# The start of a state-space and mixture-of-experts kernel: one convolution chunk moved to TensorE, three small steps moved

## The chip, the cores and the metric

The kernel is one program on one core of a Trainium2 chip. The metric is the device time of a run in microseconds. Lower is better.

## What is computed

The input x has 4 batches of 256 rows and 256 channels. It goes through a selective state-space layer (driven by a context, gated by the normalised x) with a residual, and then through a layer of 8 experts, top 2, with a residual. The part that matters here is what precedes the recurrence:

```python
x = jnp.einsum('ed,bld->bel', in_proj_w, hidden_states)      # 128 -> 256 channels
xc = conv(pad(x, 3), conv_w)                                 # 4 taps, one filter per channel
u = silu(xc + conv_b)
x_dbl = jnp.einsum('ke,bel->bkl', x_proj_w, u)               # dt_lo (8), B (16), C (16)
delta = softplus(dt_proj_w @ dt_lo + dt_proj_b)
A = -exp(A_log)
# 256 steps: state = state*exp(delta*A) + (delta*u)*B;  y = state . C
y = (y + D * u) * silu(layernorm(x))
```

The experts follow: softmax of 8 logits, top 2, capacity 320 rows for each expert, relu(rows @ w1) @ w2, weighted sum.

## The kernel before

Channels lie on the 128 partitions in two chunks (c = 0, 1), time on the free axis. Each engine has its own program, written out by hand, and runs it in order; semaphores link them. The work falls into three stages.

- The head, 0 to about 18 us: loads, and everything for batch 0 that the first scan needs.
- The scan loop, about 18 to 145 us: 32 steps (4 batches of 8 pairs of states). In step g VectorE runs `scan(g+1)` and then `mult(g)`, GpSimd makes the inputs `dbu` with `drive(g)` (the first one VectorE makes itself), ScalarE makes the decays in PSUM with `decay(g)`, and TensorE casts C with `c_cast` and adds the states up with `add_state`. Pieces of the next batches and of the routing are put between the steps at fixed places.
- The routing of the last batch, and then the experts, about 145 us to the end.

The head, in the order of its dependences. TensorE projects the context of batch 0 into two banks (L881, signalled by `xe0_psum`, one count for each chunk). VectorE waits for both and runs the four taps of both chunks, eight instructions (L1172, L1175), into `conv0`. ScalarE applies silu to chunk 0 and then chunk 1 (L608, `u_done`). TensorE multiplies `u` with `wdt`, four matmuls (`first_dt`, L765), and signals `v_psum`; `wdt` itself comes from a small product (L886), which ScalarE copies (L603). Then comes softplus for batch 0: ScalarE's Abs of both chunks (L515) and Exp (L518), the logarithm (L522); VectorE's relu (L1185), `spd` (L1188), `spt` (L1190, L1193), `delta` (L1197), `du` (L1202) and the first `dbu` (L1206). After it VectorE clears 64 rows of `xe` (L1339), runs `scan(0)` (L1227), then `lo_rows(0)` (L1153), then `scan(1)`.

`keep_clock(n, bank)` on TensorE issues n matmuls of 128 columns whose result nobody reads. In this kernel each fp32 matmul has two records in the trace. Names of banks: `WBANK` and `CBANK` hold the two projected chunks; `BBANK`, `V0BANK` and `YBANK` are others.

GpSimd in the head: it multiplies the projection into the convolution weights `cwb` for batches 1 to 3 (L333, needs `inp_in` and `cw_in`), then `z_rstd(1, ...)` with four small instructions (L320 to L328, the second is a power), the copy to `tri` (L337), eight copies into `xrow` (L339), and then `drive(1)` (L352), whose result `scan(1)` waits for.

VectorE negates `anegs` (L1182) after ScalarE has exponentiated it (L611); the decays need it. The consts tensor, 304 columns, holds the identity in its first 128 columns (`ident`) and the other constants behind it.

Of the kernel before, what the change touches and what calls it, by code (L numbers as in the profile page):

```python
# [24 lines left out]
ALU = mybir.AluOpType  # L25
ACT = mybir.ActivationFunctionType
AX = mybir.AxisListType

P = 128
B, L, DM = 4, 256, 256  # L30
DC = 128
DI, DS, TAPS, DR = 256, 16, 4, 8
EC = DI // P
# [7 lines left out]
EROWS = [min(P, CAP - t * P) for t in range(ET)]  # L41
# [6 lines left out]
CB, DSK, CONVW, ALOG = 0, 1, 2, 2 + TAPS  # L48
# [7 lines left out]
NCONST = CEND + BT * NE  # L56
# [15 lines left out]
YBANK, CBANK, BBANK, WBANK, DABANK = 0, 1, 2, 3, 4  # L72
# [18 lines left out]
def cols(b):  # L91
    return slice(b * L, (b + 1) * L)
# [10 lines left out]
def build(nc, x, ctx_t, inproj_t, xproj_t, dt_small, conv_w, chan, wg, w1, w2, consts, slot_numbers, sel,  # L103
# [4 lines left out]
    with ExitStack() as ctx:  # L108
# [53 lines left out]
        def sm(name, shape, dt=F32):  # L162
# [24 lines left out]
        zs = w2raw  # L187
        conv0 = xnt
        spe, spl, spd, spt = [w1raw[:, i // 2, (i % 2) * EC * L:(i % 2 + 1) * EC * L].rearrange("p (c t) -> p c t", c=EC)
                              for i in range(4)]  # L190
# [18 lines left out]
        def decays(r):  # L209
            return ps[:, DABANK + 2 * r:DABANK + 2 * r + 2, :]  # L210

        s = {n: ctx.enter_context(nc.semaphore(n)) for n in (
            "ones_made ctx_in0 ctx_in inp_in dts_in xps_in x_in0 x_in small_in sel_in sel_done w1_in w2_in xe_in fill_made xe_zeroed xe_filled "
            "cw_in ch_in cw_done const_done dtb_in skip_done opened weights_sum xe0_psum wdt_psum wdt_done cv_step cv_done conv_psum u_done "
# [12 lines left out]
        def _(sp):  # L227
            sp.dma_start(ctxs[:, cols(0)], ctx_t[:, cols(0)]).then_inc(s["ctx_in0"], 16)
            sp.dma_start(xps[:], xproj_t).then_inc(s["xps_in"], 16)
            sp.dma_start(xnat[:, tiles_of(0), :], x[:, tiles_of(0), :]).then_inc(s["x_in0"], 16)  # L230
            sp.dma_start(brow[0:XPC, 0:BC], sel).then_inc(s["sel_in"], 16)
            sp.dma_start(cst[:], consts).then_inc(s["small_in"], 16)
            sp.dma_start(wgs[:], wg).then_inc(s["small_in"], 16)
# [77 lines left out]
        def _(pool):  # L311
# [6 lines left out]
            def z_rstd(n, tiles):  # L318
# [10 lines left out]
                                        ).then_inc(s["z_scale"], 1)  # L329

            pool.wait_ge(s["inp_in"], 16)
            pool.wait_ge(s["cw_in"], 16)
            nc.gpsimd.tensor_tensor(cwb[:], cwb[:], inps[:, None, :].to_broadcast([P, TAPS, DI]), ALU.mult  # L333
                                    ).then_inc(s["cw_done"], 1)
            pool.wait_ge(s["small_in"], 32)
            z_rstd(1, tiles_of(0))
# [142 lines left out]
        def _(act):  # L479
            act.dma_start(inps[:], inproj_t).then_inc(s["inp_in"], 16)  # L480
            act.dma_start(ch[:], chan).then_inc(s["ch_in"], 16)
            act.dma_start(dts[:], dt_small).then_inc(s["dts_in"], 16)
            act.dma_start(cwb[:], conv_w[None, :, :].to_broadcast([P, TAPS, DI])).then_inc(s["cw_in"], 16)
# [24 lines left out]
            def decay_exps(b, bank):  # L508
                act.wait_ge(s["v_psum"], b + 1)
                if b:  # L510
                    act.wait_ge(s["delta_done"], EC * b)
                    nc.scalar.activation(spe, by_chunk(bank), ACT.Abs).then_inc(s["sp_abs"], 1)
                else:
                    for c in range(EC):
                        nc.scalar.activation(spe[:, c, :], ps[:, bank + c, 0:L], ACT.Abs,  # L515
                                             bias=ch[:, c, DTB:DTB + 1]).then_inc(s["sp_abs"], 1)
                act.wait_ge(s["sp_abs"], EC + b)
                nc.scalar.activation(spe, spe, ACT.Exp, scale=-1.0).then_inc(s["sp_exp"], 1)  # L518
# [75 lines left out]
            def split_w1(e, m):  # L594
# [5 lines left out]
                                     ).then_inc(s["w1hi_done"], 1)  # L600

            act.wait_ge(s["wdt_psum"], 1)
            nc.scalar.activation(wdt[:], ps[:, YBANK, :].rearrange("p (k d) -> p k d", k=EC), ACT.Copy  # L603
                                 ).then_inc(s["wdt_done"], 1)
            act.wait_ge(s["ch_in"], 16)
            for c in range(EC):
                act.wait_ge(s["cv_done"], c + 1)
                nc.scalar.activation(u[:, c, cols(0)], conv0[:, c, :], ACT.Silu, bias=ch[:, c, CB:CB + 1]  # L608
                                     ).then_inc(s["u_done"], 1)
            nc.scalar.preload_act_table_set(EXP_SET)  # L610
            nc.scalar.activation(anegs[:], ch[:, :, ALOG:ALOG + DS], ACT.Exp).then_inc(s["a_exp"], 1)  # L611
            act.wait_ge(s["sel_in"], 16)
            nc.scalar.activation(sels[:], brow[0:XPC, 0:BC], ACT.Copy).then_inc(s["sel_done"], 1)
            decay_exps(0, V0BANK)
            logs(0)
# [119 lines left out]
        def _(pe):  # L735
# [3 lines left out]
            def keep_clock(n, bank):  # L739

                for _ in range(n):
                    nc.tensor.matmul(ps[:, bank, 0:P], onesf[:], onesf[:], start=True, stop=True)  # L742
# [137 lines left out]
            for c, bank in ((0, WBANK), (1, CBANK)):  # L880
                nc.tensor.matmul(ps[:, bank, 0:L], inps[:, c * P:(c + 1) * P], ctxs[:, cols(0)],  # L881
                                 start=True, stop=True).then_inc(s["xe0_psum"], 1)
            keep_clock(2, BBANK)
            pe.wait_ge(s["dts_in"], 16)
# [3 lines left out]
            ins.then_inc(s["wdt_psum"], 1)  # L888
            keep_clock(6, BBANK)
            pe.wait_ge(s["wdt_done"], 1)  # L890
# [20 lines left out]
            conv(1, 1, YBANK)  # L911
            pe.wait_ge(s["small_in"], 32)
            pe.wait_ge(s["b_done"], 1)
            for c in range(KC):
# [210 lines left out]
        def _(dve):  # L1125
# [8 lines left out]
            def open_slot(r):  # L1134
                nc.vector.memset(decays(r).rearrange("p b (n t) -> p b n t", t=L)[:, :, :, 0:1], 0.0
                                 ).then_inc(s["scan_done"], 1)
# [27 lines left out]

            open_slot(0)
            dve.wait_ge(s["ch_in"], 16)
            dve.wait_ge(s["xe0_psum"], EC)
            for k, c, steps in ((0, 0, 0), (0, 1, 0), (1, 0, 1), (2, 0, 3), (1, 1, 2), (3, 0, 4), (2, 1, 5), (3, 1, 6)):
                bank = (WBANK, CBANK)[c]
                tap = ch[:, c, CONVW + TAPS - 1 - k:CONVW + TAPS - k]  # L1170
                if k == 0:
                    ins = nc.vector.tensor_scalar(conv0[:, c, :], ps[:, bank, 0:L], tap, None, ALU.mult)  # L1172
                else:
                    dve.wait_ge(s["cv_step"], steps)
                    ins = nc.vector.scalar_tensor_tensor(  # L1175
                        out=conv0[:, c, k:L], in0=ps[:, bank, 0:L - k], scalar=tap, in1=conv0[:, c, k:L],
                        op0=ALU.mult, op1=ALU.add)
                ins.then_inc(s["cv_done" if k == TAPS - 1 else "cv_step"], 1)
            dve.wait_ge(s["x_in0"], 16)
            z_variance(range(BT), z_stats(range(BT)))  # L1180
            dve.wait_ge(s["a_exp"], 1)
            nc.vector.tensor_scalar(anegs[:], anegs[:], -1.0, None, ALU.mult).then_inc(s["a_neg"], 1)  # L1182
            for c in range(EC):
# [154 lines left out]

            nc.vector.memset(xe[EROWS[2]:P, 2, :], 0.0).then_inc(s["xe_zeroed"], 1)  # L1339
            scan(0)  # L1340
# [185 lines left out]
```

## Time and profile before

| | |
|---|---|
| median of 3 runs | 294.06 us (292.55 to 295.63) |
| the profiled execution, its own time | 292.54 us |
| its span from first to last instruction | 290.7 us |
| busy: TensorE, VectorE, GpSimd, ScalarE | 83%, 76%, 77%, 60% |
| DMA | 40.38 MB, 139 GB/s mean |

The span is what the rows count in, from 0. The profiled execution is one run; its own time is its span and 1.84 us that lie outside it. "Busy" is a share of the whole span and mixes three stages with different limits.

### The profile page before, as it was taken

The numbers are of one execution on the slowest core, as the hardware profiler recorded it, in microseconds if no ns is written. First come the engines' busy times: TensorE is split into PE (matmuls) and PEld (weight loads), VectorE is DVE, ScalarE is ACT, GpSimd is POOL, SyncE is SP. The second block draws the span as 40 slices with busy tenths as digits, with TensorE's granted clock in tenths as the row PEclk, the third lists the DMA queues.
The fourth block names the chain that finished last, engine by engine and source line by source line (L and its number), as shares of the span: only waits on it lengthen the run. The fifth ranks groups of instructions, "written<-read, shape, count | busy, mean of one in ns | idle before, by whom it ended". The sixth has DMA issues, their size and how long they took to land.

```text
span 290.7 us, 4966 instructions
## 1 busy us (share of the span) xinstructions
PE 242.3 (83%) x1534; PEld 220.6 (76%) x1534; DVE 221.0 (76%) x367; ACT 175.3 (60%) x386; POOL 224.5 (77%) x180
## 2 busy tenths in 40 slices
PE   8957696596957496677898999999999999999990
PEld 7746474375845285556697898999999999999980
DVE  1799999799899999999945575848585757576710
ACT  1889657948996776669017736475655647464500
POOL 1769779879996999999951948878887878787761
PEclk9999979988999957585579999999999999999996
DMA  6569640053002804042035355365555554655120
GB/s 160 226 193 329 185 171 0 2 193 135 0 3 91 272 0 182 2 157 98 0 108 200 110 156 191 122 217 193 185 190 204 182 220 177 225 178 179 35 61 23
DMA packets 15073, 40.38 MB, mean 139 GB/s; under 512 B 2922, under 2 KB 9900, under 8 KB 12112
## 3 DMA queue, kind: packets, MB, share of 16 engines
q1 hardware_dynamic: 11792, 33.15, 33.9%
q0 software_dynamic: 2816, 6.32, 6.3%
q10 hardware_dynamic: 448, 0.70, 0.9%
q8 instruction: 8, 0.13, 0.2%
q14 instruction: 9, 0.07, 0.1%
HBM read 32.72 MB, written 8.49 MB: 142 GB/s over the span
## 4 chain that ended last, share of the span: by engine, by line
PE 39%; DVE 5%; issue 5%; POOL 3%; DMA 2%; ACT 0%; POOLq 0%; DVEq 0%
PE ps L1004 10%; PE ps L1006 10%; PE ps L1005 10%; DVE h L1227 2%; PE ps L1013 2%; DVE hc L1239 2%; PE ps L828 1%; PE ps L742 1%; POOL out L458 1%; PE ps L1020 1%; POOL so_far L449 1%; PE ps L1042 1%; DMA so_far<-out,dst 1%; DMA out<-eo,dst 1%; POOL w2lo L439 1%
## 5 line engine op out<-in xcount | busy, mean ns | idle before, releaser
L352 POOL TENSOR_TENSOR dbu<-du,bsb 128x1024 f32<-128x1024 f32 x31 | 73.6, 2392 | 2.8 <-ACT bsb L532 1.6
L546 ACT ACTIVATE ps<-delta,anegs 128x255 f32<-128x255 f32 x128 | 53.0, 462 | 12.6 <-DVE h L1220 9.3
L1411 DVE SCALAR_TENSOR_TENSOR htlo<-ps,hthi 128x320 fp32r<-128x320 f32 x64 | 30.8, 488 | 34.6 <-ACT hthi L709 26.3
L806 PE MATMUL ps<-stack,sels 64*128 64x256 f32 x64 | 18.0, 371 | 36.6 <-DVE hc L1239 33.0
L828 PE MATMUL ps<-cst,hc 128*128 128x128 f32 x256 | 45.1, 334 | 0.5 <-DVE hc L1239 0.5
L806 PEld LDWEIGHTS ps<-stack,sels 64*128 64x128 f32 x64 | 11.5, 225 | 44.3 <-issue 43.9
L439 POOL TENSOR_TENSOR w2lo<-w2raw,w2hi 128x512 fp32r<-128x512 f32 x30 | 38.7, 1318 | 6.1 <-ACT w2hi L700 6.0
L449 POOL DMA_INDIRECT so_far<-out,dst x24 | 33.1, 1380 | 12.8 <-issue 5.5
L1220 DVE TENSOR_TENSOR_SCAN h<-ps,dbu 128x1024 f32<-128x1024 f32 x18 | 41.1, 2283 | 0.6 <-issue 0.3
L828 PEld LDWEIGHTS ps<-cst,hc 128*128 128x128 f32 x256 | 36.5, 172 | 5.1 <-issue 1.8
L709 ACT ACTIVATE hthi<-ps 128x320 fp32r<-128x320 f32 x64 | 27.8, 438 | 18.6 <-PE ps L1006 14.5
L1004 PE MATMUL ps<-xthi,w1hi 128*128 (+1 forms) x120 | 37.8, 315 | 1.2 <-issue 0.7
L1239 DVE TENSOR_TENSOR hc<-h,ps 128x1024 f32<-128x1024 f32 x31 | 37.1, 1196 | 0.8 <-DVE h L1220 0.8
L1006 PE MATMUL ps<-xthi,w1lo 128*128 (+1 forms) x120 | 37.1, 309 | 0.0
L1005 PE MATMUL ps<-xtlo,w1hi 128*128 (+1 forms) x120 | 37.0, 309 | 0.0
L1004 PE MATMUL ps<-hthi,w2hi 128*128 128x320 f32 x112 | 35.2, 314 | 0.0
L1006 PE MATMUL ps<-hthi,w2lo 128*128 128x320 f32 x112 | 34.6, 309 | 0.0
L1005 PE MATMUL ps<-htlo,w2hi 128*128 128x320 f32 x112 | 34.6, 309 | 0.0
L1227 DVE TENSOR_TENSOR_SCAN h<-ps,dbu 128x512 f32<-128x512 f32 x28 | 32.7, 1208 | 1.8 <-ACT ps L546 1.8
L458 POOL DMA_INDIRECT out<-eo,dst x24 | 23.7, 988 | 6.9 <-issue 6.7
L397 POOL DMA_INDIRECT expert_rows<-xrow,sloti x16 | 16.3, 1018 | 9.8 <-ACT xrow L590 5.9
L1004 PEld LDWEIGHTS ps<-xthi,w1hi 128*128 128x128 f32 x120 | 22.5, 188 | 1.7 <-issue 0.9
(175 smaller groups left out, 526.7 us busy)
## 6 DMA issues: line engine op xcount, KB each, us to landing
w1raw<-in_w SPq DMA_DIRECT2D x8, 1024.0 KB
w2raw<-in_w SPq DMA_DIRECT2D x8, 1024.0 KB
bsb<-b_rows SPq DMA_DIRECT2D x7, 1024.0 KB, 7.2
expert_rows<-fill SPq DMA_DIRECT2D x1, 2580.0 KB, 16.0
xe<-expert_rows SPq DMA_DIRECT2D x8, 258.0 KB
out<-x SPq DMA_DIRECT2D x4, 256.0 KB, 5.2
xnat<-in_x SPq DMA_DIRECT2D x1, 768.0 KB, 7.2
xe<-expert_rows SPq DMA_DIRECT2D x8, 64.5 KB
```

The costliest lines, as they stand in the source:

```text
L352: nc.gpsimd.tensor_tensor(dbu[j % DRING][:], du[:, :, None, cols(b)].to_broadcast([P, EC, 2, L]), bsb[b % 2][:, None, 2 * p:2 * p + 2, :]. ...
L439: nc.gpsimd.tensor_tensor(w2lo[:, fs, :], w2raw[:, fs, :], w2hi[:, fs, :].bitcast(F32), ALU.subtract).then_inc(s["w2lo_done"], 1)
L449: nc.gpsimd.indirect_dma_start(so_far[0:EROWS[t], t, :], None, out, bass.IndirectOffsetOnAxis(ap=dst[0:EROWS[t], e * ET + t, :], axis=0), ...
L546: ins = nc.scalar.activation(decays(g % SLOTS_DA)[:, c, i * L + 1:(i + 1) * L], delta[:, c, b * L + 1:(b + 1) * L], ACT.Exp, scale=anegs[: ...
L828: ins = nc.tensor.matmul(y[:, t, c * P:(c + 1) * P], hc[g % SUMS][:, c, i, t * P:(t + 1) * P], ident, start=False, stop=(g % PAIRS == PAIR ...
L1004: nc.tensor.matmul(out_, hi_a, hi_b, start=start, stop=False)
L1005: nc.tensor.matmul(out_, hi_a, lo_b, start=False, stop=False)
L1006: return nc.tensor.matmul(out_, lo_a, hi_b, start=False, stop=stop)
L1220: nc.vector.tensor_tensor_scan(h[g % HRING][:].rearrange("p c n t -> p (c n t)"), decays(g % SLOTS_DA).rearrange("p c t -> p (c t)"), dbu[ ...
L1227: nc.vector.tensor_tensor_scan(h[g % HRING][:, c].rearrange("p n t -> p (n t)"), decays(g % SLOTS_DA)[:, c, :], dbu[g % DRING][:, c].rearr ...
L1239: nc.vector.tensor_tensor(hc[g % SUMS][:].rearrange("p c n t -> p c (n t)"), h[g % HRING][:].rearrange("p c n t -> p c (n t)"), ps[:, c_ba ...
L1411: nc.vector.scalar_tensor_tensor(out=htlo[:, f, :], in0=ps[:, f % 4, 0:CAP], scalar=0.0, in1=hthi[:, f, :].bitcast(F32), op0=ALU.max, op1= ...
```

## The change

- TensorE now does the taps of chunk 1 of batch 0. ScalarE copies the projected chunk from PSUM to `conv0` (`xe0_copied`), GpSimd makes four diagonal matrices out of the identity and the taps (`diag`, in the buffer of `hc[1]`, `diag_done`), and TensorE multiplies the one with the other, four matmuls into `BBANK` (`conv0_psum`). VectorE keeps the taps of chunk 0, four instructions, each waiting for the one before.
- In TensorE's order the product L886 stands ahead of the first `keep_clock`; the two fillers of 2 and 6 matmuls around it become 1 ahead of the four tap matmuls and 2 behind them, ahead of `first_dt`.
- ScalarE runs Abs and Exp of softplus ahead of the exponential of `anegs` and the rounding of `sels`, which then stand ahead of the logarithm.
- The negation of `anegs` moves from VectorE to GpSimd, behind the product for `cwb` and ahead of `z_rstd(1, ...)`; GpSimd waits there for `a_exp`.
- The clearing of 64 rows of `xe` moves from just before `scan(0)` to the start of VectorE's program.
- The identity is loaded by a DMA of its own (128 columns, third on ScalarE's queue); the load of `dts`, third there before, is now second on SyncE's queue. The rest of the constants stays where it was.

```diff
+        diag = hc[1][:].rearrange("p c n t -> p (c n) t")
...
         def _(sp):
             sp.dma_start(ctxs[:, cols(0)], ctx_t[:, cols(0)]).then_inc(s["ctx_in0"], 16)
+            sp.dma_start(dts[:], dt_small).then_inc(s["dts_in"], 16)
             sp.dma_start(xps[:], xproj_t).then_inc(s["xps_in"], 16)
...
-            sp.dma_start(cst[:], consts).then_inc(s["small_in"], 16)
+            sp.dma_start(cst[:, P:NCONST], consts[:, P:NCONST]).then_inc(s["small_in"], 16)
...
+            pool.wait_ge(s["ch_in"], 16)
+            pool.wait_ge(s["ident_in"], 16)
+            for k in range(TAPS):
+                ins = nc.gpsimd.tensor_scalar(diag[:, k, 0:P], ident, ch[:, 1, CONVW + TAPS - 1 - k:CONVW + TAPS - k], None,
+                                              ALU.mult)
+            ins.then_inc(s["diag_done"], 1)
             pool.wait_ge(s["inp_in"], 16)
             pool.wait_ge(s["cw_in"], 16)
             nc.gpsimd.tensor_tensor(cwb[:], cwb[:], inps[:, None, :].to_broadcast([P, TAPS, DI]), ALU.mult
                                     ).then_inc(s["cw_done"], 1)
+            pool.wait_ge(s["a_exp"], 1)
+            nc.gpsimd.tensor_scalar(anegs[:], anegs[:], -1.0, None, ALU.mult).then_inc(s["a_neg"], 1)
             pool.wait_ge(s["small_in"], 32)
             z_rstd(1, tiles_of(0))
...
             act.dma_start(ch[:], chan).then_inc(s["ch_in"], 16)
-            act.dma_start(dts[:], dt_small).then_inc(s["dts_in"], 16)
+            act.dma_start(ident, consts[:, 0:P]).then_inc(s["ident_in"], 16)
...
+            act.wait_ge(s["xe0_psum"], EC)
+            nc.scalar.activation(conv0[:, 1, :], ps[:, CBANK, 0:L], ACT.Copy).then_inc(s["xe0_copied"], 1)
             act.wait_ge(s["wdt_psum"], 1)
...
-            for c in range(EC):
-                act.wait_ge(s["cv_done"], c + 1)
-                nc.scalar.activation(u[:, c, cols(0)], conv0[:, c, :], ACT.Silu, bias=ch[:, c, CB:CB + 1]
-                                     ).then_inc(s["u_done"], 1)
+            act.wait_ge(s["cv_done"], 1)
+            nc.scalar.activation(u[:, 0, cols(0)], conv0[:, 0, :], ACT.Silu, bias=ch[:, 0, CB:CB + 1]
+                                 ).then_inc(s["u_done"], 1)
+            act.wait_ge(s["conv0_psum"], 1)
+            nc.scalar.activation(u[:, 1, cols(0)], ps[:, BBANK, 0:L], ACT.Silu, bias=ch[:, 1, CB:CB + 1]
+                                 ).then_inc(s["u_done"], 1)
             nc.scalar.preload_act_table_set(EXP_SET)
+            decay_exps(0, V0BANK)
             nc.scalar.activation(anegs[:], ch[:, :, ALOG:ALOG + DS], ACT.Exp).then_inc(s["a_exp"], 1)
             act.wait_ge(s["sel_in"], 16)
             nc.scalar.activation(sels[:], brow[0:XPC, 0:BC], ACT.Copy).then_inc(s["sel_done"], 1)
-            decay_exps(0, V0BANK)
             logs(0)
...
-            keep_clock(2, BBANK)
             pe.wait_ge(s["dts_in"], 16)
...
             ins.then_inc(s["wdt_psum"], 1)
-            keep_clock(6, BBANK)
+            keep_clock(1, V0BANK)
+            pe.wait_ge(s["xe0_copied"], 1)
+            pe.wait_ge(s["diag_done"], 1)
+            for k in range(TAPS):
+                ins = nc.tensor.matmul(ps[:, BBANK, k:L], diag[:, k, 0:P], conv0[:, 1, 0:L - k], start=(k == 0),
+                                       stop=(k == TAPS - 1))
+            ins.then_inc(s["conv0_psum"], 1)
+            keep_clock(2, V0BANK)
             pe.wait_ge(s["wdt_done"], 1)
...
             open_slot(0)
+            nc.vector.memset(xe[EROWS[2]:P, 2, :], 0.0).then_inc(s["xe_zeroed"], 1)
             dve.wait_ge(s["ch_in"], 16)
-            dve.wait_ge(s["xe0_psum"], EC)
-            for k, c, steps in ((0, 0, 0), (0, 1, 0), (1, 0, 1), (2, 0, 3), (1, 1, 2), (3, 0, 4), (2, 1, 5), (3, 1, 6)):
...
+            dve.wait_ge(s["xe0_psum"], 1)
+            for k in range(TAPS):
...
             dve.wait_ge(s["x_in0"], 16)
             z_variance(range(BT), z_stats(range(BT)))
-            dve.wait_ge(s["a_exp"], 1)
-            nc.vector.tensor_scalar(anegs[:], anegs[:], -1.0, None, ALU.mult).then_inc(s["a_neg"], 1)
...
-            nc.vector.memset(xe[EROWS[2]:P, 2, :], 0.0).then_inc(s["xe_zeroed"], 1)
             scan(0)
```

## Rows read from the trace of the kernel before

**Rows 1.** windows by stage: start and end, us; busy time (instructions) of each engine; granted clock; DMA

```profile
18.10:45.00 26.90, 18.97 (x101) 15.06 (x101) 26.71 (x33) 20.98 (x47) 21.93 (x12) 0.94 0.71 226
...
162.00:284.70 122.70, 120.28 (x852) 119.70 (x852) 79.67 (x157) 66.56 (x137) 96.81 (x80) 1.00 0.49 167
```

**Rows 2.** the timeline, TensorE in the head: start, duration, line, tiles, instructions merged

```profile
3.75 2.07 PE L881 MATMUL ps<-ctxs,inps 128*128 128x256 f32 x4
...
5.61 0.72 PE L742 MATMUL ps<-onesf 128*128 128x128 f32 x4
...
6.26 1.13 PE L886 MATMUL ps<-dts 8*128 8x256 f32 x4
...
7.32 1.60 PE L742 MATMUL ps<-onesf 128*128 128x128 f32 x12
...
9.26 1.97 PE L765 MATMUL ps<-u,wdt 128*128 128x256 f32 x8 [0.33 <-ACT u L608]
```

**Rows 3.** the timeline, VectorE and ScalarE between 6 and 24 us

```profile
6.74 2.68 DVE L1175 SCALAR_TENSOR_TENSOR xnt<-ps,ch,xnt 128x255 f32<-128x255 f32 x6
...
9.45 0.51 ACT L608 ACTIVATE u<-xnt,ch 128x256 f32<-128x256 f32 x1 [0.33 <-DVE xnt L1175]
9.98 1.28 ACT L610 ACT_TABLE_LOAD   x1
...
11.53 0.81 ACT L515 ACTIVATE w1raw<-ps,ch 128x256 f32<-128x256 f32 x2
...
12.37 0.63 ACT L518 ACTIVATE w1raw<-w1raw 128x512 f32<-128x512 f32 x1
...
13.41 0.68 DVE L1190 TENSOR_TENSOR w1raw<-w1raw 128x512 f32<-128x512 f32 x1
...
16.47 1.23 DVE L1206 TENSOR_TENSOR dbu<-du,bsb 128x1024 f32<-128x1024 f32 x1
...
17.81 0.27 DVE L1339 MEMSET xe<- 64x258 f32 x1
18.11 2.34 DVE L1227 TENSOR_TENSOR_SCAN h<-ps,dbu 128x512 f32<-128x512 f32 x2
...
20.48 0.42 DVE L1153 TENSOR_TENSOR stack<-ps,stack 32x256 fp32r<-32x256 f32 x1
...
20.93 2.34 DVE L1227 TENSOR_TENSOR_SCAN h<-ps,dbu 128x512 f32<-128x512 f32 x2
```

**Rows 4.** the timeline, one DMA issue on ScalarE's queue

```profile
1.66 0.58 ACTq L482 DMA_DIRECT2D dts<-in_dt_small  x1
```

**Rows 5.** DMA issues up to 40 us: size, us from issue to landing

```profile
xps<-in_xproj_t SPq DMA_DIRECT2D x1, 64.0 KB, 2.7
...
brow<-in_sel SPq DMA_DIRECT2D x1, 8.0 KB, 6.6
```

**Rows 6.** the timeline, GpSimd in the head

```profile
8.76 2.35 POOL L333 TENSOR_TENSOR cwb<-cwb,inps 128x1024 f32<-128x1024 f32 x1 [7.35 <-DMA cwb<-in_conv_w]
...
11.38 0.73 POOL L322 TENSOR_TENSOR rz<-vz,nhalf 128x2 f32<-128x2 f32 x1
...
12.66 0.29 POOL L337 CAST tri<-cst 128x128 bf16<-128x128 f32 x1
...
12.90 2.18 POOL L339 COPY xrow<-cst 128x2 f32<-128x2 f32 x8
...
16.66 3.23 POOL L352 TENSOR_TENSOR dbu<-du,bsb 128x1024 f32<-128x1024 f32 x1 [1.58 <-ACT bsb L532]
```

**Rows 7.** the timeline of 14.5 to 14.7 us, uncut pieces

```profile
14.19 0.72 DVE L1193 TENSOR_TENSOR w1raw<-w1raw 128x512 f32<-128x512 f32 x1
...
14.31 0.65 POOL L339 COPY xrow<-cst 128x2 f32<-128x2 f32 x1
```

**Rows 8.** groups by line and form, GpSimd: count, busy us, mean ns, idle before

```profile
L352 POOL TENSOR_TENSOR dbu<-du,bsb 128x1024 f32<-128x1024 f32 x31 | 73.6, 2392 | 2.8 <-ACT bsb L532 1.6 <-DMA bsb<-b_rows 1.0
...
L359 POOL TENSOR_SCALAR w1raw<-w1raw 128x512 f32<-128x512 f32 x3 | 5.8, 1941 | 1.7 <-ACT w1raw L518 1.5
```

More of the change, by code:

```diff
@@ L212, in build @@
         s = {n: ctx.enter_context(nc.semaphore(n)) for n in (
-            "ones_made ctx_in0 ctx_in inp_in dts_in xps_in x_in0 x_in small_in sel_in sel_done w1_in w2_in xe_in fill_made xe_zeroed xe_filled "
+            "ident_in diag_done xe0_copied conv0_psum ones_made ctx_in0 ctx_in inp_in dts_in xps_in x_in0 x_in small_in sel_in sel_done w1_in w2_in xe_in fill_made xe_zeroed xe_filled "
             "cw_in ch_in cw_done const_done dtb_in skip_done opened weights_sum xe0_psum wdt_psum wdt_done cv_step cv_done conv_psum u_done "
@@ L912, in _ @@
             pe.wait_ge(s["small_in"], 32)
+            pe.wait_ge(s["ident_in"], 16)
             pe.wait_ge(s["b_done"], 1)
@@ L1165, in _ @@
             open_slot(0)
+            nc.vector.memset(xe[EROWS[2]:P, 2, :], 0.0).then_inc(s["xe_zeroed"], 1)
             dve.wait_ge(s["ch_in"], 16)
-            dve.wait_ge(s["xe0_psum"], EC)
-            for k, c, steps in ((0, 0, 0), (0, 1, 0), (1, 0, 1), (2, 0, 3), (1, 1, 2), (3, 0, 4), (2, 1, 5), (3, 1, 6)):
-                bank = (WBANK, CBANK)[c]
-                tap = ch[:, c, CONVW + TAPS - 1 - k:CONVW + TAPS - k]
+            dve.wait_ge(s["xe0_psum"], 1)
+            for k in range(TAPS):
+                tap = ch[:, 0, CONVW + TAPS - 1 - k:CONVW + TAPS - k]
                 if k == 0:
-                    ins = nc.vector.tensor_scalar(conv0[:, c, :], ps[:, bank, 0:L], tap, None, ALU.mult)
+                    ins = nc.vector.tensor_scalar(conv0[:, 0, :], ps[:, WBANK, 0:L], tap, None, ALU.mult)
                 else:
-                    dve.wait_ge(s["cv_step"], steps)
+                    dve.wait_ge(s["cv_step"], k)
                     ins = nc.vector.scalar_tensor_tensor(
-                        out=conv0[:, c, k:L], in0=ps[:, bank, 0:L - k], scalar=tap, in1=conv0[:, c, k:L],
+                        out=conv0[:, 0, k:L], in0=ps[:, WBANK, 0:L - k], scalar=tap, in1=conv0[:, 0, k:L],
                         op0=ALU.mult, op1=ALU.add)
```

## The prediction

> **What bounds the kernel now.** I read the busy times by stage first, because the change touches only the head. In the first 27 us of the scan loop VectorE is busy 26.71 of 26.90 us, and in the experts TensorE is busy 120.28 of 122.70 us [rows 1]. Neither stage has a hole that could swallow a shift of the head, and neither gets less work from this change. So what the change is worth is the shift of one event, the start of scan(1) on VectorE, at 20.93 us [rows 3]; from there on the old order of work runs, late or early by that much. One scan earlier, scan(0) starts at 18.11.
>
> Then I read the timeline of the head, engine by engine, and looked for what ends last ahead of that event. On TensorE the projection runs from 3.75 to 5.82, fillers from 5.61, the small product from 6.26, fillers from 7.32, and first_dt from 9.26 to 11.23 [rows 2]. On ScalarE the second silu ends at 9.96, the table load at 11.26, Abs starts at 11.53, and Exp ends at 13.00; VectorE then goes almost without a break from 13.41 to the end of the first dbu at 17.70, clears xe for 0.27 us, starts scan(0) at 18.11, ends it at 20.45, and runs lo_rows (0.42 us) before scan(1) [rows 3]. The head's path is therefore: taps on VectorE, silu, first_dt on TensorE, softplus, du, dbu, the memset, scan(0), lo_rows. GpSimd runs beside it: the cwb product 8.76 to 11.11, the power at 11.38, the copies up to 15.08, then drive(1) from 16.66 to 19.89 [rows 6], 1.04 us before scan(1) needs it.
>
> **Part 1: the taps on two engines.** VectorE's instructions go at one for each 0.45 us (six in 2.68) [rows 3]; chunk 0 alone needs four, some 2 us, and can start before the second projection has ended. So silu 0 is ready by about 7.5 and isn't late for anything. Chunk 1 is now the question, and with it TensorE's order.
>
> TensorE: the small product can start at 5.61, where the fillers stood, and occupies 1.06 us (6.26 to 7.32); one filler costs 1.60/6 = 0.27. It stands ready for the taps at 5.61 + 1.06 + 0.27 = 6.94 [rows 2]. ScalarE's copy of chunk 1 costs about what a silu of that size does, 0.51 [rows 3], and is done at 5.82 + 0.1 + 0.5 = 6.4, in time.
>
> GpSimd: the four diagonals need the identity. It is issued where dts was, at 1.66 [rows 4]. A load of its size and shape (64 KB, 128 rows of 512 bytes) landed 2.7 us after its issue; a small one (8 KB) issued a little later took 6.6 us, because it stood behind 256 KB on SyncE's queue [rows 5]. Nothing large stands ahead of the identity on ScalarE's queue, so I take 1.66 + 2.7 = 4.4. No row has a one-operation multiplication by a per-partition scalar on GpSimd with 128 columns. From below: the 128-column cast, 0.29 [rows 6]. From above: a quarter of the 512-column two-operation instruction, 1.94/4 = 0.49 [rows 8], plus a fixed part of at most 2.18/8 = 0.27, a two-column copy [rows 6], so 0.76. I take 0.6, nearer to the tensor-scalar row. Four are done at 4.5 + 2.4 = 6.9 (5.7 to 7.5). The taps start at 7.0 (6.94 to 7.6).
>
> From there the path is TensorE alone: four tap matmuls like first_dt's, 1.8 us until the next can start (1.97 with the tail), two fillers 0.53, then first_dt 1.97 [rows 2]: v_psum at 7.0 + 4.3 = 11.3, where it was at 11.23. Silu 1 lies beside the fillers and the first half of first_dt: taps done at 9.0, silu done at 9.7, second half of first_dt due at about 10.2. The path is no shorter: four matmuls have taken the place of four VectorE instructions, and they no longer overlap with the wait for silu 0.
>
> **Part 2: softplus first.** Between the end of first_dt and Abs lay 0.30 us, in which ScalarE finished the table load and issued two small instructions [rows 2, 3]. Now Abs follows v_psum by 0.1: at 11.4, a gain of 0.13 (0.2 to a loss of 0.5 by the bounds above). The two small ones stand ahead of the logarithm; delta needs that only after three more VectorE instructions of 0.46 to 0.72 us, so they cost nothing, with some 0.8 us of cover.
>
> **Part 3: the memset.** From the end of the first dbu to scan(0) lay 0.41 us, of which 0.27 was the memset [rows 3]. At the start of VectorE's program it lies in an idle stretch. With 0.05 left for the hand-over it gains 0.36. The negation of anegs had slack on VectorE and gains nothing there.
>
> Sum up to scan(0): a gain of 0.13 + 0.36 = 0.5 us, scan(0) at 17.6, and scan(1) wanted at 20.44.
>
> **Part 4: GpSimd's new wait.** It waits for a_exp in front of a queue: the negation, four instructions of z_rstd, the cast, eight copies, and drive(1), which scan(1) waits for. a_exp comes after Exp, at about 13.1; the queue used to start at 11.11 and took 3.97 us up to 15.08 [rows 6]. With the negation (0.25) it is through at 17.3 at the earliest, against a start of drive(1) at 16.66.
>
> And it will be slowed. A two-column copy issued 0.12 us after VectorE's subtraction of two SBUF operands took 0.65 us and ended 0.05 after it [rows 7]; drive(1), beside such an instruction for 1.04 us, took 3.23 where the mean is 2.39 [rows 6, 8]. Before, only two such VectorE instructions fell on GpSimd's queue. Now all from L1190 to L1206 do, from 13.3 to 17.6 [rows 3], and the small ones get through in the gaps, one or two in each of five. I expect four to six of the copies behind the dbu, at some 0.15 each: drive(1) starts at 18.2 (17.3 to 18.8). With no dbu of VectorE beside it, it takes 2.39 and ends at 20.6 (19.7 to 21.2). The other direction counts as well: a GpSimd instruction let into a gap holds up VectorE's next one, 0.1 to 0.6 us in sum; I take 0.2, which moves scan(1)'s own readiness to 20.6 too.
>
> **Sum.** scan(1) at 20.7 against 20.93: a gain of 0.2 us (bounds: a gain of 0.8, a loss of 1.3). The profiled execution would go from 292.54 to 292.3. It lay 1.52 below the median of the runs, within their spread of 3 us; on the median, 294.06 - 0.2 = 293.9.
>
> The Trainium skill, "SBUF — State Buffer", section "Who interferes with whom", says that a VectorE instruction with two SBUF inputs and a GpSimd instruction that reads SBUF exclude one another for the whole of whichever came first. By that rule the copies above are explained, the trace agrees with it in this direction; the other direction, VectorE held by GpSimd, no row here shows at any length. What it would make of the power is rival B.
>
> **Rival A: GpSimd isn't in the way.** If its queue is through near 17.3 and VectorE isn't held, drive(1) ends at 19.7, scan(1) goes when lo_rows is done, and with cheap diagonals the gain is 0.5 to 0.8: 293.4. For it: the small instructions did get through in pairs between two subtractions. Against it: five more of these VectorE instructions than before.
>
> **Rival B, slower: the power holds VectorE.** The power takes 0.73 us for two columns [rows 6]. If it is let in ahead of one of delta, du or dbu and keeps the operand path until it ends, VectorE's path grows by 0.6, the dbu ends at 17.8 to 18.2, and seven or eight copies (1.3 us) come behind it: drive(1) 19.5 to 21.9, a loss of 1.0: 295.1. It decides once drive(1) starts after 18.5. For it: the power stands second in the queue, exactly when VectorE begins its run.
>
> **Rival C, slower: the identity is late.** If it lands with the crowd, at 1.66 + 6.6 = 8.3 like the 8 KB load, the taps start at 10.8, and 3.7 us are lost less what the memset gives: 297.4. It costs from a landing at about 4.6 on, one for one. Against it: the short queue ahead of it.
>
> **Rival D: it is not the head that decides.** The granted clock is 1.00 over the experts [rows 1]; another phase of it in the stages before could move the end by 1% either way, as the runs of before differ by that.
>
> **How the numbers follow.** Forecast 0.54 (293.9, its own range 293.4 to 294.5), A 0.22 (293.4), B 0.16 (295.1), C 0.04 (297.4), D 0.04 (291 or 297). Three runs of before span 292.55 to 295.63, so about 1% is what this kernel's measurement can tell from no change. The range takes in A and B and half of that spread: 292.4 to 295.6. Faster by over 1% needs 2.9 us, which no part of the head has to give: 0.04. Slower by over 1% is C and half of D: 0.06. Same: 0.90.
>
> **What the profile would show.** Part 1: tap matmuls on TensorE starting near 7.0, v_psum's last matmul ending near 11.3; a start after 7.6 means that diagonals or identity were dearer. Part 2: Abs at 11.4, 0.1 behind it. Part 3: no memset ahead of scan(0). Part 4: GpSimd idle after the cwb product until 13.1, copies stretched beside VectorE, drive(1) starting near 18.2 and lasting 2.4, scan(1) at 20.7, waiting for GpSimd or ready with it. The prediction is wrong if scan(1) starts before 20.1 or after 22.2, or if the shift at scan(1) is not the shift at the end.

## The result and the profile after

The changed kernel takes 299.69 us in the median of 4 runs (296.96 to 301.1), the kernel before 293.31 in the same series (292.11 to 295.63). The ratio is 1.0201 with a 95% interval of 1.0156 to 1.0247: slower by about 2%, 6.4 us, where 0.2 us less was forecast. The profiled execution took 301.10 us, its span 298.8. It is the slowest of the four, and the profiled execution of the kernel before (292.54) the second fastest of its four, so the two spans lie 8.1 us apart, more than the medians. Runs over 1.5% above the fastest of their kernel are left out of the ratios, here and below: none of these, but two of e2's four, three of e1's ten (297.5, 297.7 and 755 us), four of e5's twelve (297.3 to 297.8), one of e11's twelve (297.3) and two of the kernel before (296.4 and 326.5).

The head first, by the timeline of the changed kernel (start, duration, engine, line; in brackets the idle time ahead and what ended it).

```profile
5.71 1.26 PE L899 MATMUL ps<-dts 8*128 8x256 f32 x4
...
6.90 0.49 PE L756 MATMUL ps<-onesf 128*128 128x128 f32 x2
...
7.38 2.38 POOL L336 TENSOR_SCALAR hc<-cst,ch 128x128 f32<-128x128 f32 x4 [5.98 <-DMA cst<-in_consts]
...
9.91 3.40 PE L906 MATMUL ps<-xnt,hc 128*128 128x256 f32 x8 [2.52 <-POOL hc L336]
...
13.59 1.89 PE L779 MATMUL ps<-u,wdt 128*128 128x256 f32 x8
...
15.52 0.84 ACT L525 ACTIVATE w1raw<-ps,ch 128x256 f32<-128x256 f32 x2 [0.40 <-PE ps L779]
...
17.40 0.69 DVE L1209 TENSOR_TENSOR w1raw<-w1raw 128x512 f32<-128x512 f32 x1
...
18.26 1.21 POOL L324 TENSOR_TENSOR rz<-vz,nhalf 128x2 f32<-128x2 f32 x1
...
18.92 0.76 DVE L1216 TENSOR_TENSOR delta<-w1raw 128x256 f32<-128x256 f32 x2
...
20.44 1.22 DVE L1225 TENSOR_TENSOR dbu<-du,bsb 128x1024 f32<-128x1024 f32 x1
20.45 1.36 POOL L347 CAST tri<-cst 128x128 bf16<-128x128 f32 x1
...
21.70 2.34 DVE L1246 TENSOR_TENSOR_SCAN h<-ps,dbu 128x512 f32<-128x512 f32 x2
```

GpSimd waits 5.98 us for the identity and starts the diagonals at 7.38, not at 4.5. TensorE has done its filler at 7.39 and stands still for 2.52 us; the taps start at 9.91. They take 3.40 us where four matmuls of this size take 1.89 a little later (line 779). The rest follows in the old distances: the first dbu starts at 20.44, where it was 16.47 [rows 3], and scan(0) comes 0.04 us after its end, without the memset. It starts at 21.70, 3.59 later than before.

The landing is in the view of the DMA issues (size, us from issue to landing):

```profile
xps<-in_xproj_t SPq DMA_DIRECT2D x1, 64.0 KB, 2.7
cst<-in_consts ACTq DMA_DIRECT2D x1, 64.0 KB, 5.5
```

The 64 KB of xps, issued at 1.59 and third on SyncE's queue, still landed 2.7 us after the issue; the identity, of the same size, issued 0.07 us later and third on ScalarE's queue, took 5.5. The windows of the changed kernel show what the clock did (busy time of each engine, then the granted clock, 1.00 being 2.4 GHz and 0.50 being 1.2):

```profile
8.00:9.80 1.80, 0.00 (x0) 0.00 (x0) 0.57 (x2) 0.00 (x0) 1.80 (x5) 0.90 1.02 364
9.90:13.00 3.10, 3.09 (x8) 2.55 (x9) 0.34 (x3) 0.00 (x0) 2.17 (x1) 0.52 0.75 297
34.00:37.00 3.00, 3.00 (x11) 1.52 (x10) 2.00 (x2) 0.35 (x3) 2.69 (x2) 0.54 0.24 62
```

Nothing on TensorE from 8.0 to 9.8, then the taps at 0.52. The third row is a second place of that kind.

Further on in the timeline of the changed kernel, the start of scan(1) and two rows of batch 1:

```profile
25.15 2.34 DVE L1246 TENSOR_TENSOR_SCAN h<-ps,dbu 128x512 f32<-128x512 f32 x2 [0.66 <-POOL dbu L362]
...
34.65 1.97 PE L759 MATMUL ps<-u,xps 128*64 128x256 f32 x4
...
37.32 0.42 DVE L1174 TENSOR_TENSOR stack<-ps,stack 32x256 fp32r<-32x256 f32 x1 [1.32 <-ACT stack L510]
```

scan(1) starts 0.66 us late for GpSimd's drive(1). The projection for batch 1, at the lower level, takes 1.97 us; the same four records took 1.08 in the head at the upper one. So VectorE waits 1.32 for the rows copied from it. The rows of the head show why drive(1) is late: beside VectorE's run the power takes 1.21 us (0.73 alone [rows 6]) and the cast 1.36 (0.29), while VectorE's two delta instructions, beside the power, take the usual 0.76 together.

The whole difference of the spans, 8.1 us, by the starts of VectorE's instructions in the two traces: 3.6 up to scan(0), 0.6 from there to scan(1), 1.3 more at mult(3) (the wait just shown), 1.3 more at mult(13), and 1.25 between the last mult and the end. At mult(13) the profile names no releaser; VectorE starts as soon as the cast of C (line 820) is done, and that stands behind a convolution and the logits at the lower level:

```profile
77.60 3.60 PE L786 MATMUL ps<-ctxs,cwb 128*128 128x256 f32 x8
...
80.99 1.02 PE L868 MATMUL ps<-wgs,xnt 128*128 128x8 f32 x8
81.94 0.50 PE L820 MATMUL ps<-stack,sels 64*128 64x256 f32 x2
...
82.53 1.22 DVE L1258 TENSOR_TENSOR hc<-h,ps 128x1024 f32<-128x1024 f32 x1 [1.97 <-issue]
```

The trace of the kernel before has such a convolution at this place too (3.46 us), and a wait of 0.80.

### The profile page after: what moved, and what is told of

It reads as the page before. It is cut to its first block, busy times and chain, and to the rows that moved or that the text cites. A ratio compares the mean times of both kernels' runs of the same rounds, so it can differ in the third digit from the quotient of the medians.

```text
span 298.8 us, 4966 instructions
## 1 busy us (share of the span) xinstructions
PE 251.2 (84%) x1532; PEld 226.5 (76%) x1532; DVE 218.1 (73%) x362; ACT 175.6 (59%) x387; POOL 227.3 (76%) x185
## 4 chain that ended last, share of the span: by engine, by line
PE 41%; POOL 24%; issue 17%; DVE 7%; DMA 5%; ACT 4%; POOLq 1%; ACTq 0%; SPq 0%; DVEq 0%
PE ps L1025 10%; PE ps L1027 10%; PE ps L1026 10%; POOL dbu L362 8%; DVE hc L1258 3%; POOL expert_rows L407 2%; POOL w1raw L369 2%; DVE h L1239 2%; DMA cst<-in_consts 2%; PE ps L1034 2%; PE ps L842 1%; POOL delta L380 1%; POOL du L384 1%; POOL w1raw L375 1%; POOL out L468 1%
## 5 line engine op out<-in xcount | busy, mean ns | idle before, releaser
L362 POOL TENSOR_TENSOR dbu<-du,bsb 128x1024 f32<-128x1024 f32 x31 | 72.7, 2363 | 0.3
L820 PE MATMUL ps<-stack,sels 64*128 64x256 f32 x64 | 18.7, 383 | 33.0 <-DVE hc L1258 30.3
L820 PEld LDWEIGHTS ps<-stack,sels 64*128 64x128 f32 x64 | 12.1, 237 | 41.4 <-issue 40.7
```

What stands on the lines that cost most here:

```text
L362: nc.gpsimd.tensor_tensor(dbu[j % DRING][:], du[:, :, None, cols(b)].to_broadcast([P, EC, 2, L]), bsb[b % 2][:, None, 2 * p:2 * p + 2, :]. ...
```

## The experiments

Times of the head are from the one profiled execution of each kernel; the ratio is against the kernel before, run in the same series on the same chip. "Tail" is the time from the last mult to the end of the span.

| kernel | taps: start, us | scan(0) | scan(1) | last mult | tail | ratio (95%) |
|---|---|---|---|---|---|---|
| before | | 18.11 | 20.93 | 144.70 | 146.0 | 1 |
| changed | 9.91, 3.40 | 21.70 | 25.15 | 151.55 | 147.3 | 1.0201 (1.0156 to 1.0247) |
| e1 identity on SyncE | 6.75, 1.96 | 17.09 | 20.54 | 146.94 | 145.8 | 1.0047 (0.9998 to 1.0096) |
| e2 12 fillers | 12.99, 2.25 | 23.64 | 27.08 | 152.23 | 147.5 | 1.015 (1.0034 to 1.0267) |
| e3 before, memset | | 19.49 | 22.30 | 148.22 | 145.8 | 0.9967 (0.9933 to 1.0000) |
| e4 negation on ScalarE | 9.20, 3.58 | 21.16 | 23.98 | 147.83 | 147.4 | 1.0166 (1.0094 to 1.0237) |
| e5 e1 and e4 | 6.53, 1.88 | 16.83 | 19.65 | 143.47 | 147.2 | 1.0000 (0.9967 to 1.0034) |
| e6 before, small moves | | 17.52 | 20.33 | 144.28 | 148.0 | 0.9995 (0.9964 to 1.0026) |
| e7 x later | 8.12, 3.64 | 20.16 | 23.61 | 150.06 | 147.4 | 1.0178 (1.0102 to 1.0255) |
| e8 5 fillers | 9.54, 3.55 | 21.49 | 24.94 | 151.31 | 147.4 | 1.0235 (1.0174 to 1.0296) |
| e9 10 fillers | 8.53, 1.88 | 18.80 | 22.25 | 147.07 | 145.9 | 1.0129 (1.0091 to 1.0167) |
| e10 before, loads | | 18.04 | 20.86 | 146.25 | 145.8 | 0.9989 (0.9952 to 1.0026) |
| e11 e5 and tail fillers | 6.75, 1.96 | 17.08 | 19.89 | 144.46 | 145.7 | 0.9955 (0.9918 to 0.9992) |
| e12 before, tail fillers | | 18.02 | 20.84 | 146.71 | 145.8 | 0.9974 (0.9949 to 0.9999) |
| e13 cwb later | 8.63, 3.73 | 21.69 | 25.14 | 149.92 | 145.9 | one run, 298.04 us |
| e14 x and cwb later | 8.33, 3.60 | 21.22 | 24.67 | 149.47 | 145.9 | one run, 297.71 us |
| e15 identity ahead of ch | 9.35, 3.61 | 21.36 | 24.80 | 151.22 | 147.6 | one run, 301.03 us |

**The place of the identity (e1).**

```diff
+            sp.dma_start(ident, consts[:, 0:P]).then_inc(s["ident_in"], 16)
             sp.dma_start(dts[:], dt_small).then_inc(s["dts_in"], 16)
...
-            act.dma_start(ident, consts[:, 0:P]).then_inc(s["ident_in"], 16)
```

> The changed kernel with one DMA moved: the identity is issued second on SyncE's queue (1.18 us) and no longer third on ScalarE's. Theory 1, the late identity is the cause: a load of 64 KB from that place landed 2.7 us after its issue, so it lands near 3.9, the diagonals run from 4.2 to 6.6, the taps start near 7.0 and take 1.9 us, scan(0) starts near 17.6 (it was 21.70, before the change 18.11) and the time is near that of before, 293 us. Theory 2, the diagonals or the new order cost it wherever the load stands: scan(0) stays above 20 and the time above 298.

The timeline of e1: diagonals, taps, scan(0) and scan(1).

```profile
4.22 2.38 POOL L337 TENSOR_SCALAR hc<-cst,ch 128x128 f32<-128x128 f32 x4 [2.81 <-DMA ch<-in_chan]
...
6.75 1.96 PE L906 MATMUL ps<-xnt,hc 128*128 128x256 f32 x8
...
17.09 2.34 DVE L1246 TENSOR_TENSOR_SCAN h<-ps,dbu 128x512 f32<-128x512 f32 x2
...
20.54 2.34 DVE L1246 TENSOR_TENSOR_SCAN h<-ps,dbu 128x512 f32<-128x512 f32 x2 [0.66 <-POOL dbu L363]
```

The diagonals wait for the channel constants now, not for the identity, which landed 2.8 us after its issue. TensorE has no gap and the taps run at the upper level. scan(0) starts at 17.09, a microsecond ahead of the old kernel's. Theory 1 holds: with one DMA moved the ratio is 1.0047, where it was 1.0201. GpSimd's wait ahead of scan(1) is as before, 0.66 us.

**The negation (e4).**

```diff
-            pool.wait_ge(s["a_exp"], 1)
-            nc.gpsimd.tensor_scalar(anegs[:], anegs[:], -1.0, None, ALU.mult).then_inc(s["a_neg"], 1)
...
             nc.scalar.activation(sels[:], brow[0:XPC, 0:BC], ACT.Copy).then_inc(s["sel_done"], 1)
+            act.wait_ge(s["a_exp"], 1)
+            nc.scalar.activation(anegs[:], anegs[:], ACT.Copy, scale=-1.0).then_inc(s["a_neg"], 1)
```

> The changed kernel with the negation of anegs on ScalarE (behind sels) and GpSimd's wait for a_exp gone. Theory, GpSimd's new wait holds scan(1): GpSimd goes on from its cwb product at 12.1, its small instructions lie ahead of VectorE's run, drive(1) starts as soon as its casts are there (20.8 in place of 22.77) and scan(1) follows lo_rows without a wait, 0.66 us earlier against scan(0). The time falls by 0.7 us. Rival, something else held drive(1): the gap of 0.66 us ahead of scan(1) stays.

The timeline of e4: the power, drive(1), scan(1).

```profile
12.43 0.72 POOL L324 TENSOR_TENSOR rz<-vz,nhalf 128x2 f32<-128x2 f32 x1
...
20.40 2.94 POOL L360 TENSOR_TENSOR dbu<-du,bsb 128x1024 f32<-128x1024 f32 x1 [5.42 <-ACT bsb L540]
...
23.98 2.34 DVE L1246 TENSOR_TENSOR_SCAN h<-ps,dbu 128x512 f32<-128x512 f32 x2
```

The power is at 12.43 and takes 0.72, drive(1) starts at 20.40 in place of 22.77, and scan(1) follows scan(0) by 2.82 us in place of 3.45. So the wait cost 0.63 us where it stood. The ratio, 1.0166, is too close to 1.0201 for the intervals to tell apart, so the 0.7 us expected in the time is not shown.

**Both repairs (e5).**

> The changed kernel with both repairs: the identity second on SyncE's queue, the negation on ScalarE. If the late load and GpSimd's wait are the two losses of the head, scan(0) starts near 17.1 us and scan(1) near 19.9, 1.0 us earlier than before the change (20.93), and the first mult near 22.2 (23.18). In the time this is a gain of 0.3% at most, unless the stretches at the 1.2 GHz level come in other places and take it back, as they did in the run with the early identity alone (0.4 us early at the first mult, 2.2 us late at the last). Rival: something else comes last ahead of scan(1), the decays or the casts, and it stays near 20.5.

scan(1) starts at 19.65, 1.28 us before the old kernel's (1.0 expected), and this lead holds to the last mult (1.23). The ratio is 1.0000 all the same, and the medians of all runs are 294.16 and 293.24. In the profiled execution the lead went in the tail, 147.2 us against 146.0. The windows of e5 show where:

```profile
150.00:155.00 5.00, 3.74 (x33) 3.46 (x32) 3.16 (x16) 4.59 (x14) 0.00 (x0) 0.64 0.90 292
155.00:160.00 5.00, 5.00 (x27) 5.00 (x26) 0.98 (x2) 0.87 (x2) 3.56 (x4) 0.67 0.30 111
```

The windows of e11, which has fillers there:

```profile
150.00:155.00 5.00, 4.89 (x53) 4.52 (x53) 3.38 (x19) 3.30 (x11) 0.94 (x2) 1.00 0.63 191
155.00:160.00 5.00, 5.00 (x37) 4.91 (x36) 1.93 (x9) 2.42 (x8) 2.04 (x2) 1.00 0.43 164
```

In e5 TensorE was busy 3.74 of 5 us, and the level is 0.64 and 0.67; the first expert starts in it. In e11 it was busy 4.89, and the level stays at 1.00. But it stays there without fillers as well. The kernel before, at the same place:

```profile
150.00:155.00 5.00, 4.56 (x50) 3.95 (x47) 3.14 (x18) 3.27 (x10) 0.95 (x2) 1.00 0.65 188
```

And e10, which has no fillers either, and whose last mult is 2.8 us later than e5's:

```profile
154.00:159.00 5.00, 3.89 (x41) 3.46 (x40) 3.15 (x16) 4.93 (x16) 0.00 (x0) 1.00 0.87 304
```

**Fillers in the tail (e11, and e12 as its control).**

```diff
             counts(B - 1)
+            keep_clock(6, DABANK)
             pe.wait_ge(s["xe_zeroed"], 1)
```

> The repaired kernel (identity second on SyncE's queue, negation on ScalarE) with six more fillers on TensorE behind the counts of the last batch, where it stood idle for 1.3 us waiting for the rows of the first expert. From the last mult to the end the repaired kernel took 147.2 us, the kernel before 146.0; the difference was a stretch at the lower level from 151.4 to 158.2. If idle time there brings the level down, the fillers keep it up, the tail takes 146 us and the median comes under that of before by the 1.2 us that the head gained (292.0). Rival: the level falls anyway at that place, the tail stays at 147.2, and the fillers give nothing.

> The control: the kernel before with the same six fillers. If they help only where the level would fall, the median comes down by less than 0.5 us here; if they help in every run, by as much as in the repaired kernel, and then the repair and the fillers are two separate gains.

e11 has the lowest ratio of the study, 0.9955 (0.9918 to 0.9992), with 292.29 us in the median of 12 runs (290.35 to 297.3); the control has 0.9974 (0.9949 to 0.9999). Both tails were 145.7 to 145.8. That the fillers made them so is not shown: of the 15 traces without these fillers seven have a tail of 145.8 to 146.0 (before, e1, e3, e9, e10, e13, e14) and eight one of 147.2 to 148.0, so a single trace with a short tail could be chance. The two intervals overlap and the control's ends at 0.9999, so how much of e11's 0.45% is the fillers' and how much the head's isn't settled.

**Fillers ahead of the taps (e2, e8, e9)**: 12, 5 and 10 in place of 1.

> The changed kernel with 12 filler matmuls in place of 1 ahead of the taps, so that TensorE isn't idle from 7.4 to 9.9 us while it waits for the diagonals. Theory 1, the identity is late and the clock fell on top of it: the taps still start near 9.9, but take 1.9 us where they took 3.4; scan(0) moves from 21.70 to 20.2. The time falls by 1.5 us if the later slow stretches stay as they are. Rival, the slow taps have another cause than the idle stretch (the form of the weights, say): they take 3.4 us again and scan(0) stays at 21.7.

> The changed kernel with 5 filler matmuls ahead of the taps in place of 1 (12 were too many in the run before, where TensorE was at the lower level until 13.8 us). They cover the wait for the diagonals in part, and end before it does. If the idle stretch brought the clock down, the taps take 1.9 us in place of 3.4 and scan(0) starts at 20.2 or, with the load as late as in the other runs, at 19.5; the time is 1.5 us lower than the changed kernel's. Rival: the taps take 3.4 us again.

> The changed kernel with 10 fillers ahead of the taps in place of 1, as 5 left TensorE idle for 1.3 us and the taps again took 3.55. At the upper level ten take 2.4 us and end near 9.3, when the diagonals are there. If any idle of over a microsecond ahead of the taps brought the level down, the taps now take 1.9 us, scan(0) starts near 20.0 and the time is 1.5 us under the changed kernel's, near 298. Rival: the level has nothing to do with the idle time and the taps take 3.5 us.

The windows ahead of the taps and in them, for e8:

```profile
8.00:9.50 1.50, 0.23 (x3) 0.03 (x1) 0.00 (x0) 0.00 (x0) 1.40 (x3) 0.96 0.97 354
9.60:12.60 3.00, 3.00 (x7) 2.43 (x8) 1.00 (x4) 0.00 (x0) 2.35 (x1) 0.50 0.81 322
```

And for e9:

```profile
8.00:9.50 1.50, 1.50 (x12) 1.40 (x11) 0.00 (x0) 0.00 (x0) 0.07 (x1) 1.00 1.02 357
9.60:12.60 3.00, 3.00 (x17) 2.72 (x16) 1.00 (x4) 1.76 (x2) 2.35 (x1) 1.00 0.80 320
```

e2 told nothing: by its durations TensorE was at the lower level up to its taps in that execution (the small product took 2.07 us in place of 1.13, the twelve fillers 5.5 us); the column of the granted clock, which says 1.00 there, doesn't show it. e8 and e9 tell more. With 5 fillers TensorE stands idle for 1.32 us and the taps run at 0.50, 3.55 us long. With 10 it isn't idle and they run at 1.00, 1.88 long. The other traces agree: the taps took 3.40 to 3.73 us in all six with an idle stretch of 1.3 to 2.5 us ahead of them (changed, e4, e7, e8, e13, e15), and 1.88 to 1.96 in the four without one whose small product took 1.1 (e1, e5, e9, e11). The idle stretch is what slowed the taps, by 1.7 us between e8 and e9. In e9's execution the identity had also landed after 3.8 us in place of 5.5, so only a part of its 2.9 us at scan(0) is the level's.

**The small moves and the loads, on the old taps (e3, e6, e10).**

> The kernel before with the clearing of xe alone moved to the start of VectorE's program. By the prediction's step: scan(0) follows the first dbu by 0.1 us in place of 0.41 and starts near 17.8, and the time falls by 0.3 us, which three rounds may not tell. Rival, scan(0) waits for the decays anyway: it stays at 18.1.

> The kernel before with the small moves alone: memset at the start, softplus ahead of the small instructions, the negation on ScalarE; taps, loads and GpSimd's order as before. By the prediction's parts 2 and 3 scan(0) starts 0.5 us earlier against first_dt's end than before the change (6.88 us after it before, 6.4 now) and the time falls by 0.5 us. Rival, the small instructions ahead of the logarithm hold delta: the distance stays at 6.9.

> The kernel before with the changed kernel's loads alone (identity third on ScalarE's queue, dts second on SyncE's, the constants in two pieces), taps and order as before. If the late identity costs only because the taps wait for it, this is as fast as before (within 0.3 us), with scan(0) at 18.1, as nothing else needs the identity before 20 us. Rival: the rearranged loads hold the head up by themselves (projection, small product), and scan(0) starts above 19.

e3: scan(0) follows the dbu by 0.04 us (it was 0.41), so the memset gives what it was said to. Its head was late for another reason, in two rows of the timeline of e3:

```profile
7.25 1.13 PE L886 MATMUL ps<-dts 8*128 8x256 f32 x4 [1.39 <-DMA dts<-in_dt_small]
...
8.31 2.92 PE L742 MATMUL ps<-onesf 128*128 128x128 f32 x12
```

Here dts, in the very place that the identity took, came so late that TensorE idled for 1.39 us, and the fillers behind ran at half speed (2.92 us, 1.60 in [rows 2]). e3's loads are those of the kernel before, so that kernel has the same weak place; in its profiled execution dts was there in time. e6: from the end of first_dt to scan(0) 6.35 us in place of 6.88, the 0.5 of parts 2 and 3; no change of the time can be told. e10: scan(0) at 18.04, and no loss, though the identity took 5.2 us. The late landing costs only because the taps wait for it.

**What holds the third load (e7, e13, e14, e15).** e7 moved x for batch 0 (256 KB) behind the constants, e13 moved cwb (512 KB), e14 both, e15 swapped the identity with the channel constants.

> The changed kernel with the load of x for batch 0 (256 KB) moved on SyncE's queue behind the constants; the identity stays third on ScalarE's queue. If x crowds the identity out, the identity lands near 4.5 in place of 7.2, the diagonals are done near 7.0 and scan(0) starts near 18. If the taps' weights for the other batches (512 KB, right behind on the same queue) or the place itself do it, it lands at 6.5 to 7.3 again and scan(0) stays above 20.

> The changed kernel with the load of the taps' weights for the other batches (512 KB, issued right behind the identity on ScalarE's queue) moved to SyncE's queue behind the constants. With the identity third on ScalarE's queue and these loads around it, it landed 5.5, 4.7, 4.8, 5.2 and 3.8 us after its issue in five kernels. If these 512 KB keep it, it lands about 2.8 after its issue, as in the second place of SyncE's queue, and the taps start near 7. If x on the other queue does, it stays at 3.8 to 5.5.

> Both large loads, x for batch 0 and the 512 KB, moved behind the constants on SyncE's queue; the identity stays third on ScalarE's. If bytes in flight around it are the reason in either form, it lands about 2.8 us after its issue and scan(0) starts near 17.5. If the third place itself, or the time at which it is issued, is late by some other reason, it stays at 3.8 to 5.5.

> The changed kernel with the identity second on ScalarE's queue and the channel constants (23 KB) third. If what is issued third, at 1.66 us, falls into the crowded time and what is issued at 1.18 does not, the identity lands about 2.8 us after its issue and the channel constants, which the taps and the diagonals need as well, are late in its place: scan(0) stays above 20. If only large loads are late, both land by 4.5 and scan(0) starts near 17.5.

The landing of the identity in e14, in the view of the DMA issues:

```profile
cst<-in_consts ACTq DMA_DIRECT2D x1, 64.0 KB, 3.0
```

And of the identity and the channel constants in e15:

```profile
cst<-in_consts ACTq DMA_DIRECT2D x1, 64.0 KB, 3.1
...
ch<-in_chan ACTq DMA_DIRECT2D x1, 23.0 KB, 5.1
```

With the loads as in the changed kernel the identity took 5.5, 4.7, 4.8, 5.2, 3.8 and 5.2 us (changed, e2, e4, e8, e9, e10). With x or cwb alone moved it took 3.8 and 4.3, which that spread covers. With both moved it took 3.0. Issued second it took 3.1, and then the 23 KB of channel constants, third, took 5.1 in place of 2.9. So it isn't the load's size and not its own queue, but the time of its issue, as long as the two large loads are there. On SyncE's queue it is the same: xps, issued at 1.59, took 2.5 to 3.3 us in every kernel with the changed loads, and in e1, where it is issued at 2.06, 5.0:

```profile
xps<-in_xproj_t SPq DMA_DIRECT2D x1, 64.0 KB, 5.0
```

Why 0.07 us between 1.59 and 1.66 makes 2.8 us is open. The part on the large loads rests on one execution for e14 and e15 each. In none of the last three did the time come down (297.7 to 301.0 us): in e14 TensorE was, by its durations, at the lower level through most of the taps (small product 2.07 us, taps 3.60), in e13 idle for 2.25 us ahead of them, and in e15 the channel constants were waited for.

## Why the prediction was wrong, step by step

- **What bounds the kernel, and the event to watch.** Right for the head; wrong in "the shift of one event is the change's worth". The shift at scan(1), 4.2 us, is half of the 8.1 between the two traces and two thirds of the 6.4 between the medians; in e5 a lead of 1.23 us at the last mult was worth nothing in the median. The loop and the tail hold places where TensorE is the last one as soon as its clock is at the lower level. Where such stretches fall changes from one execution to the next even with the same code: up to the tail e12 is the kernel before, and its last mult starts at 146.71, not 144.70. The forecast had this as rival D with 0.04 and no mechanism.
- **Part 1, the identity.** This step failed. I took 1.66 + 2.7 = 4.4 from a load of the same shape issued half a microsecond earlier, and put the late landing at 0.04 (rival C, 8.3). It landed at 7.2. Rival C had the mechanism; its time was still 2.3 us short of the median. The argument "nothing large stands ahead of it on its queue" was the wrong question: the large loads beside it and behind it were in flight too. My own row of the small load with 6.6 us showed how a crowded time looks, and I had that wrong too: it is not only what stands ahead of it, as with the 256 KB behind it (e7) it still took 4.4, and only with both large loads moved (e14) 2.8.
- **Part 1, the diagonals.** Four took 2.38 us, 0.6 each, as taken. With the identity early the taps started at 6.75 (forecast 7.0).
- **Part 1, the taps' price.** 1.8 at the upper level was right (1.88); 3.40 was measured, as the wait for the diagonals was 2.5 us of idle TensorE. I costed the late load "one for one" and gave no price to what the idle time does to the clock. Late identity and slow taps together make 4.4 us against my 7.0 and 1.9.
- **Parts 2 and 3.** Right: 0.5 us in e6, 0.04 behind the dbu in every kernel with the memset moved.
- **Part 4, GpSimd's wait.** The mechanism was right and the size nearly: drive(1) started 1.07 after scan(0) (forecast 0.6), took 2.34 (2.39), and scan(1) waited 0.66; taking the wait away gave 0.63. The other direction was wrong for the head: I let GpSimd hold VectorE for 0.2 us, but from the start of the first two-input instruction to the end of the dbu VectorE took 4.26 us in the changed kernel (17.40 to 21.66) and 4.29 before [rows 3]. Rival B's mechanism, the power holding VectorE, didn't occur. Elsewhere in these traces GpSimd does hold VectorE (last section).

So the sum of the head, as argued, was right within 0.5 us once the identity is early. That e1's scan(1) is nearer still (20.54, forecast 20.7) is luck: scan(0) came 0.5 early (17.09, forecast 17.6), and the step to scan(1) took 3.45 us where 3.1 was forecast. What was missing in the trace: 2.9 us of waiting, 1.5 of slow taps, and 3.9 later on.

Shown by runs: the place of the identity, the idle time as the reason of the slow taps, GpSimd's wait. Only read from traces: that the lower level makes the losses at mult(3), mult(13) and in the tail. Open: why these stretches fall where they do, and how much of the 3.9 us the change brings about at all. In the profiled executions mult(3) comes 1.0 to 1.5 us late against mult(0) in eight of the nine kernels with GpSimd's wait ahead of scan(1) (not in e2), but also in e3, e10 and e12, which have no such wait; e12's code there is that of the kernel before.

## What to carry to other kernels

A load of which something critical is to be made needs the landing time of its own place in the issue order, read with all that is in flight beside it; a load of the same size issued earlier, even 0.07 us earlier, says nothing. Where a step is moved to TensorE behind a wait, its price has two values (here 1.9 and 3.4 us), and idle time ahead of it can bring the higher one: have the operand early, or fill that time. A gain of 1.2 us in the head can be lost again in a later stage, so look at the granted clock of every stage before taking a shift of one event for the result, and at more than one execution before giving a late stretch to the change.

## What had not been expected of the hardware

- Idle stretches on TensorE of 1.3 us (e7, e8) and 2.5 us (changed) were followed by taps at the lower level. A longer one, from about 17.6 to 21.0, was followed by it in one execution and not in another, though the code up to there is the same. The kernel before, and then e12, which differs from it only in the tail:

```profile
21.45 1.98 PE L772 MATMUL ps<-ctxs,cwb 128*128 128x256 f32 x8
```

```profile
21.65 3.76 PE L772 MATMUL ps<-ctxs,cwb 128*128 128x256 f32 x8
```

- In the head GpSimd was held by VectorE's instructions with two SBUF operands (0.29 us became 1.36), and VectorE was not held by GpSimd's power over two columns: beside one of 1.21 us its own took 0.38 each, as always. With longer GpSimd instructions VectorE is held as well. Two rows of the experts, in the kernel before:

```profile
183.91 1.32 POOL L439 TENSOR_TENSOR w2lo<-w2raw,w2hi 128x512 fp32r<-128x512 f32 x1
```

```profile
184.50 2.54 DVE L1336 TENSOR_TENSOR w1lo<-w1raw,w1hi 128x512 fp32r<-128x512 f32 x1
```

VectorE's subtraction, 0.59 us behind GpSimd's first of two, took 2.54 us where the three after it took 0.68 each, and ended 0.55 after GpSimd's second. The Trainium skill, "SBUF — State Buffer", section "SBUF: two separate sides", has the pair taken for the whole instruction by whichever comes first. The trace agrees with it here, and with the cast in the head; the power in the head, which VectorE did not wait for, it doesn't explain.
- The same load in the same place took 3.8 to 5.5 us in six kernels.
